# A gated cross-attention and mixture-of-experts block: routing and dispatch of the first mixture placed between the heads of the attention ahead of it

## The chip, the cores and the metric

One core of a Trainium2 chip runs the whole program. The time is device microseconds (us) of one execution; smaller is better. The kernel before took 1334.66 us in the median of three runs (1333.32 to 1339.74). Engines are called PE (matrix product), DVE (vector), ACT (scalar), POOL (GpSimd) and SP (which issues most DMAs).

## What is computed

The input `x` is 2048 tokens of 256 numbers (8 sequences of 256), with 512 context rows of 128. Four blocks follow each other, each added to `x` with a gate:

```python
x = x + tanh(g_xattn[0]) * L0_xattn(layernorm(x), ctx)   # 16 heads of 128, q and k RMS-normed, 64 keys a sequence
x = x + tanh(g_ffn[0])   * L0_ffn(layernorm(x))          # 64 experts, 8 per token, and a shared MLP
x = x + tanh(g_xattn[1]) * L1_xattn(layernorm(x), ctx)
x = x + tanh(g_ffn[1])   * L1_ffn(layernorm(x))          # 8 experts, every token through all
```

The change concerns the first two. The routing of `L0_ffn`, for each token, and the places of its rows at the experts:

```python
scores = sigmoid(x @ router.T); sc = scores + e_bias      # 64 experts in 8 groups
group_scores = top_k(sc by group, 2).sum(-1)              # best 4 of the 8 groups stay
topk_idx = top_k(masked sc, 8); topk_w = 2.5 * scores[topk_idx] / their sum
pos = running count of tokens per expert, in token order  # valid where pos < CAP
buf[expert, pos] = x[token]                               # [64, CAP, 256]
y = silu(buf @ w_gate) * (buf @ w_up) @ w_down            # per expert, inner size 88
out[token] += y[expert, pos] * topk_w;   out += shared_mlp(x)
```

CAP is 128 and the 2048 tokens make 256 choices per expert on average, so the places are filled by the earlier tokens, and most choices of the later half find none.

## The kernel before

The 2048 tokens lie in 16 tiles of 128 (partition = token), in 4 groups of 4 tiles. **First attention.** One step per group, i = 0 to 3. In a step PE goes through 16 heads: queries of the head (L1664, six 128x512 products in the split fp32r form), their squares summed for the norm (L1640), scores (L1649). DVE copies the queries out of PSUM (L707); ACT squares and rounds them; POOL subtracts to get the low part `q_lo` (L468), which L1640 reads. The softmax of the group before (DVE L641 to L664, exp on ACT) lies between the heads, and so does its product with the values (L1619). At the end of a step, behind head 15, PE computes for the next group the keys (L1555), the values times `Wo` (L1583, 32 products of 128x256), the token transposes (L1592) and the transposes of the normed keys (L1563). DVE copies the keys (L604), squares them (L610) and sums the squares (L612). The steps are a loop; the order inside one is written out by hand, and every engine follows it through ring counters (a bank of PSUM is filled, read, given back).

**First mixture.** After step 3 the rest of the attention of group 3 and the layer norms are done, then, group by group, the router logits, the routing on DVE (about L779 to L876, each operation over 4 tiles at once, 128x256), and the shared MLP on PE (L1708, L1728). The normed rows and the 64 weights of each token go to a table in DRAM (L379). The places of the tokens are then found per expert from keys: `largest` (L901, L904) takes the 8 greatest of a row of keys and strikes them out, 16 times over 1024 keys and 16 times over 256 candidates. Index arithmetic gives `src_now` and `dst_now`. The experts follow: 8 steps of 4 quarters q, 2 experts in each. For a quarter SP loads `w_gu`, `w_dn` (L383, L384), POOL gathers the 128 rows of each expert from the table (L479, an indirect DMA per expert), PE transposes them (L1750) and multiplies (L1764, L1777), ACT and DVE work between, and POOL adds the results to sums in DRAM (L489, an accumulating indirect DMA per expert). An accumulating DMA waits for the one before it to the same sum to have landed; there are two sums. When all are added, SP loads the sums (L418) and the second attention starts; from there on the two programs are alike.

## Time and profile before

| | |
|---|---|
| median of three runs | 1334.66 us (1333.32 to 1339.74) |
| the profiled execution, its own time | 1336.93 us |
| span in its profile | 1335.2 us |
| busy over the span | PE 1038.4 us (78%), DVE 697.9 (52%), ACT 431.5 (32%), POOL 278.2 (21%) |
| bytes moved by DMA | 66.36 MB |
| chain that ended last | PE 54%, DVE 14%, issue 12%, DMA 6%, ACT 6%, POOL 6% |

The stages of the span, as the views of the trace give them: up to 33.6 us first loads and preparation; heads of steps 0 to 3 from 33.6, 100.4, 186.6 and 272.6, each followed by its step's end; 337 to 470 the rest of the attention, routing, shared MLP; 470 to 530 the places; 543.0 the first addition to the sums and 744.2 the first load of them; from there the second attention and the second mixture up to 1335 us. An average over the span mixes these, so each part of the change has to be read in its own stage.

### The profile page before, as it was taken

To read this page: it belongs to the slowest core of one execution; us is meant where nothing else is said; L and a number is where in the kernel's file an instruction comes from. 1 tells how busy PE (TensorE), PEld (TensorE's weight loads), DVE (VectorE), ACT (ScalarE), POOL (GpSimd) and SP (SyncE) were. 2 spreads that over 40 slices of the span, in tenths; PEclk is the share of its full clock that TensorE was granted. 3 is DMA by queue.
4 is the path that set the end of the run, shared out by engine and by line. 5 is a ranking of instruction groups with operands and counts; after the bars stand their busy time and mean duration, and the time that the engine had idled before them with its cause. 6 is when DMAs were issued, how large, how long until landed. Compare 5 with 4: busy or idle time off the path is not lost.

```text
span 1335.2 us, 16322 instructions
## 1 busy us (share of the span) xinstructions
PE 1038.4 (78%) x5301; PEld 855.8 (64%) x5301; DVE 697.9 (52%) x1659; ACT 431.5 (32%) x793; POOL 278.2 (21%) x223
## 2 busy tenths in 40 slices
PE   5989979989766400776667368887989999999997
PEld 3867858778545300665556226564657989898996
DVE  6277586675758897222223477575675324232221
ACT  4565465554623100111111032324252232322221
POOL 0414214133000001788787110010100000000000
PEclk8999999999887655888787566757666999899899
DMA  7004000000001040788786540000000000000001
GB/s 266 3 0 137 1 1 1 0 1 1 1 0 40 24 126 11 170 173 180 166 186 120 144 164 1 2 0 0 0 0 0 1 1 0 0 0 0 0 0 64
DMA packets 58967, 66.36 MB, mean 50 GB/s; under 512 B 5037, under 2 KB 55719, under 8 KB 58151
## 3 DMA queue, kind: packets, MB, share of 16 engines
q1 hardware_dynamic: 45268, 46.48, 11.1%
q0 software_dynamic: 12288, 18.88, 8.1%
q8 instruction: 28, 0.46, 0.1%
q10 hardware_dynamic: 1363, 0.37, 0.1%
q14 instruction: 20, 0.16, 0.0%
HBM read 48.13 MB, written 17.56 MB: 49 GB/s over the span
## 4 chain that ended last, share of the span: by engine, by line
PE 54%; DVE 14%; issue 12%; DMA 6%; ACT 6%; POOL 6%; ACTq 0%; DVEq 0%; POOLq 0%; SPq 0%
PE bank L1959 12%; PE bank L1978 7%; DMA acc<-y,dst_now 5%; PE bank L1619 4%; PE bank L1664 4%; PE bank L1887 3%; PE bank L1845 3%; PE bank L1649 3%; POOL acc L489 2%; PE bank L1970 2%; POOL xg L479 2%; PE bank L1904 2%; POOL q_lo L468 2%; DVE cand L901 1%; PE bank L1804 1%
## 5 line engine op out<-in xcount | busy, mean ns | idle before, releaser
L1959 PE MATMUL bank<-gu_hi,xnT_split 128*128 128x352 f32 x640 | 158.7, 328 | 0.0
L468 POOL TENSOR_TENSOR q_lo<-soft,q_hi 128x512 fp32r<-128x512 f32 x64 | 93.2, 1456 | 236.8 <-ACT soft L1313 236.7
L1959 PEld LDWEIGHTS bank<-gu_hi,xnT_split 128*128 128x128 f32 x640 | 112.6, 190 | 1.0 <-issue 0.7
L479 POOL DMA_INDIRECT xg<-table,src_now x64 | 63.9, 999 | 216.5 <-DVE src_now L927 197.4
L489 POOL DMA_INDIRECT acc<-y,dst_now x64 | 102.3, 1599 | 26.7 <-issue 20.3
L1959 PE MATMUL bank<-gu_lo,xnT_split 128*128 128x352 f32 x320 | 103.8, 324 | 0.0
L1183 DVE SCALAR_TENSOR_TENSOR soft<-sg,combine_w,bank 128x176 f32<-128x176 f32 x160 | 56.4, 395 | 87.4 <-PE bank L1959 81.3
L1978 PE MATMUL bank<-dn,attnT 128*128 128x256 f32 x448 | 101.2, 384 | 0.0
L1978 PEld LDWEIGHTS bank<-dn,attnT 128*128 128x128 f32 x448 | 85.6, 194 | 11.2
L707 DVE COPY qT<-bank 128x512 f32<-128x512 f32 x64 | 44.2, 691 | 87.7 <-PE bank L1664 86.6
L1517 ACT ACTIVATE sg<-bank 128x352 f32<-128x352 f32 x80 | 37.1, 464 | 152.0 <-PE bank L1959 151.9
L947 DVE TENSOR_SCALAR y<-bank,xg 128x256 f32<-128x256 f32 x64 | 28.0, 480 | 106.6 <-PE bank L1777 106.6
L627 DVE SCALAR_TENSOR_TENSOR x<-bank,gates,x 128x256 f32 (+1 forms) x48 | 22.7, 482 | 114.0 <-PE bank L1978 94.8
L1764 PEld LDWEIGHTS bank<-xgT,w_gu 128*88 128x88 f32 x512 | 75.8, 193 | 6.7 <-issue 3.8
L1764 PE MATMUL bank<-xgT,w_gu 128*88 128x128 f32 x512 | 77.3, 316 | 0.7 <-issue 0.7
L1750 PE MATMUL bank<-ident,xg 128*128 128x128 f32 x128 | 25.7, 335 | 65.5 <-DMA xg<-table,src_now 65.5
L1309 ACT ACTIVATE q_hi<-qT 128x512 fp32r<-128x512 f32 x64 | 40.4, 630 | 91.3 <-DVE qT L707 91.2
L1619 PE MATMUL bank<-vw,attnT 128*128 128x256 f32 x256 | 62.1, 399 | 4.3 <-ACT attnT L1263 4.3
L1649 PE MATMUL bank<-kT,qT 128*128 128x64 f32 x512 | 64.0, 268 | 0.0
L1649 PEld LDWEIGHTS bank<-kT,qT 128*128 128x128 f32 x512 | 62.5, 191 | 1.4
L1750 PEld LDWEIGHTS bank<-ident,xg 128*128 128x128 f32 x128 | 17.4, 169 | 70.1 <-DMA xg<-table,src_now 56.5
L1959 PEld LDWEIGHTS bank<-gu_lo,xnT_split 128*128 128x128 f32 x320 | 60.7, 190 | 0.3
(256 smaller groups left out, 2140.1 us busy)
## 6 DMA issues: line engine op xcount, KB each, us to landing
w_gu<-in_L_ffn_w_gu SPq DMA_DIRECT2D x32, 352.0 KB
w_dn<-in_L_ffn_w_down SPq DMA_DIRECT2D x32, 176.0 KB
acc<-zeros SPq DMA_DIRECT2D x2, 2176.0 KB, 11.4
acc_rows<-acc SPq DMA_DIRECT2D x8, 512.0 KB, 4.9
gu<-in_L_gu SPq DMA_DIRECT2D x1, 3520.0 KB, 13.7
table<-xw SPq DMA_DIRECT2D x4, 640.0 KB
wo<-in_L_xattn_Wo SPq DMA_DIRECT2D x2, 1024.0 KB, 16.2
wq<-in_L_xattn_Wq SPq DMA_DIRECT2D x1, 2048.0 KB, 18.5
```

Of the source, the lines that this page charges most:

```text
L468: pool.tensor_tensor(q2_lo[:, h % 3, :], q2[h % 2], q2_hi[:, h % 3, :], ALU.subtract).then_inc(q2_split, 1)
L479: pool.indirect_dma_start(xg[:, q, e, :], None, table, bass.IndirectOffsetOnAxis(ap=src_now[:, q, e:e + 1], axis=0)).then_inc(xg_loaded[q] ...
L489: pool.indirect_dma_start(acc[e], bass.IndirectOffsetOnAxis(ap=dst_now[:, q, e:e + 1], axis=0), y[:, q, e, :], None, compute_op=ALU.add).t ...
L707: dve.tensor_copy(qT[:, h % 3, :], qr.read(dve)[:]).then_inc(q_ring.free, 1)
L1183: ins = dve.scalar_tensor_tensor(out=act_v[:, j % 2, at:at + F1], in0=sg[:, (j + p) % 2, e * F1:(e + 1) * F1], scalar=combine_w[:, j, 2 * ...
L1619: mm = pe.matmul(o_banks[0][:, 0:DIM], attnT[:, j % 2, p, :], vw[:, j // 2, p, :], start=(p == 0), stop=(p == 7))
L1649: mm = pe.matmul(s_bank[0][:, at:at + SKV], qT[:, h % 3, j * P:(j + 1) * P], kT[:, h, (j // 2) * SKV:(j // 2 + 1) * SKV], start=True, stop ...
L1664: mm = pe.matmul(b[:], w[:, c, h * D0:(h + 1) * D0], v[:, c, :], start=(n == 0), stop=(n == len(terms) - 1))
L1750: mm = pe.transpose(b[:, at:at + P], xg[:, q, e, c * P:(c + 1) * P], ident[:])
L1764: mm = pe.matmul(b[0:I0, e * P:(e + 1) * P], w_gu[:, q, e, c, o:o + I0], xgT[:, q % 2, e, c, :], start=(c == 0), stop=(c == C - 1))
L1959: mm = pe.matmul(b[:, 0:2 * F1], v[:, c, j * P:(j + 1) * P], w[:, c, p, o, :], start=(n == 0), stop=(n == len(terms) - 1))
L1978: mm = pe.matmul(o_banks[j % 2][:, 0:DIM], attn_flat[0:n, f, :], dn1[0:n, f, :], start=(f == 0), stop=(f == FC - 1))
```

## The change

The work of routing and of sending rows moves into steps 1 to 3 of the first attention, in batches of tiles (`BATCHES`: [0], [1,2], [3,4], ... [13,14], [15]), as soon as a tile's attention is done.

- **Routing** on DVE works on one or two tiles (128x64 or 128x128 per operation) in pieces `ln_*`, `choose1`, `choose2`, `choose3`, `place`, put between the softmax pieces at given heads (`ROUTE_EARLY`, `ROUTE_LATE`). Batches 0 to 4 are so treated in steps 1 to 3 (the last place of them behind step 3), batches 5 to 8 after step 3.
- **Places**: for each tile PE multiplies the chosen-expert matrix by a triangular matrix (`earlier`), plus ones times what earlier tiles took. DVE turns this into 8 row numbers per token, in a table of 64 x 128 rows. `largest` and the index arithmetic go.
- **Sending**: POOL stores the 128 rows of a tile 8 times, each by an indirect DMA of 128 rows x 1284 B: 128 stores in all. A row carries the normed token, the 64 weights and the token's number. In the program's order 24 stand in step 2, 21 in step 3, 83 behind it. A choice that found no place gets a row number beyond the table, which the store leaves out. Before a second use of its slots, `place` waits for the stores of two batches ago, and tiles from the ninth on share a counter with the tile 8 before. The table (10.5 MB) is filled with zeros first, by four DMAs of SP from step 0 on.
- **Experts**: no gathers. SP loads the 2 x 128 rows of a quarter by one ordinary DMA, 4 quarters ahead; the token number in the row gives the destination of the addition. The weights are laid out so that a partition's part lies in one piece in DRAM (2816 and 2048 B, where it was 704 and 1024 B). The accumulating DMAs stay as they are.
- **Steps**: the values move from the step's end into heads 0, 1, 3 and 5 of the next step (now read out of PSUM by ACT), the key transposes behind head 1. ACT takes the squares of the keys, reading PSUM, with a sum; L604, L610, L612 go. `q_lo` and its partner have two buffers where they had three. The steps are written out, not a loop.
- **Shared MLP**: after the last `place`, in products 512 wide; its inputs are stored to DRAM and loaded back transposed by SP.

```diff
-ROW = DIM + E0
+TOKEN = DIM + E0
+ROW = TOKEN + 1
...
+BATCHES = [[0]] + [[2 * n - 1, 2 * n] for n in range(1, NT // 2)] + [[NT - 1]]
...
+def early(i):
+    return 2 * (i - 1)
+def late(i):
+    return 2 * i - 1
...
+ATTN_TURNS, ATTN_OUTS, VALUE_TURNS = {5: 0, 8: 1, 12: 2, 15: 3}, {6: 0, 9: 1, 13: 2}, {0: 0, 1: 2, 3: 4, 5: 6}
...
+            if i and h == 1:
+                keys_across(i)
+            if i and h in ATTN_TURNS:
+                attn(i - 1, ATTN_TURNS[h])
+            if h >= 2 and h % 2 == 0:
+                s.append(("scores", i, (h - 2) // 2))
+            if i and h in VALUE_TURNS:
+                values(i - 1, VALUE_TURNS[h], 2)
+            if h == 7 and i + 1 < NG:
+                context(i + 1)
+            if i >= 2 and h == 7:
+                t.append(("place", late(i - 1)))
+            if i >= 2 and h == 0:
+                t.extend([("rows", late(i - 1)), ("place", early(i - 1))])
+            if i >= 2 and h == 2:
+                t.append(("logits", late(i - 1)))
+            if i and h == 11:
+                t.append(("rows", early(i)))
+            if i and h == 13:
+                t.append(("logits", early(i)))
+        if i + 1 < NG:
+            tokens(i + 1)
+        s.append(("scores", i, 7))
+        if i + 1 < NG:
...
-        table = nc.dram_tensor("table", (T + 1, ROW), F32, kind="Internal").ap()
+        table = nc.dram_tensor("table", (E0 * CAP, ROW), F32, kind="Internal").ap()
...
+            sp.wait_ge(q_ring.full, q_turn.at["query", 0, 6] + 1)
+            sp.wait_ge(blank_ready, 2)
+            table_d = table.rearrange("(e p) r -> p e r", p=P)
+            for n in range(4):
+                each = E0 // 4
+                sp.dma_start(table_d[:, n * each:(n + 1) * each, :], blank.unsqueeze(1).to_broadcast(
+                    [P, each, ROW])).then_inc(blank_stored, 16)
...
+            sp.wait_ge(s_ring.full, s_turn.at["scores", NG - 1, 7] + 1)
+            load_shared(0)
+            load_shared(1)
+            for q in range(4):
+                load_experts(0, q)
+            store_normed(5)
+            store_normed(6)
+            load_shared(2)
+            store_normed(7)
+            store_normed(8)
+            load_shared(3)
+            for n in range(8):
+                sp.wait_ge(row_stored[n], 16 * K0 * 2)
+            for q in range(4):
+                load_rows(0, q)
             for e in done1.values():
...
-                    sp.wait_ge(y_full, 4 * i + q - 3)
+                    sp.wait_ge(y_ready, 4 * i + q - 3)
+                    load_rows(i, q)
                     load_experts(i, q)
...
+            def split_squares(i, h):
+                pool.wait_ge(q2_ready, H0 * i + h + 1)
+                if H0 * i + h >= 2:
+                    pool.wait_ge(normed_head, H0 * i + h - 1)
+                pool.tensor_tensor(q2_lo[:, h % 2, :], q2[h % 2], q2_hi[:, h % 2, :],
+                                   ALU.subtract).then_inc(q2_split, 1)
...
+            def send_rows(b, lo, n):
+                for at in range(lo, min(lo + n, K0 * len(BATCHES[b]))):
+                    j, k = at // K0, at % K0
+                    t = BATCHES[b][j]
+                    pool.sem_inc(pool_wait_done, 1)
+                    pool.indirect_dma_start(table, bass.IndirectOffsetOnAxis(ap=slots[:, b % 2, j, k:k + 1], axis=0),
+                                            rows(t), None, bounds_check=E0 * CAP - 1,
+                                            oob_is_err=False).then_inc(row_stored[t % 8], 16)
...
+            FIRST, AFTER = {2: 1, 3: 2, 4: 1, 5: 2, 6: 2, 7: 2, 8: 1, 9: 2, 10: 2, 11: 1}, {12: 1, 13: 2, 14: 1, 15: 1}
+            for i in range(NG):
+                sent = {0: 0, 1: 0}
                 for h in range(H0):
-                    pool.wait_ge(q2_ready, H0 * i + h + 1)
-                    pool.tensor_tensor(q2_lo[:, h % 3, :], q2[h % 2], q2_hi[:, h % 3, :],
-                                       ALU.subtract).then_inc(q2_split, 1)
-
-            with pool.Fori(0, NG) as i:
-                split_squares(i)
+                    split_squares(i, h)
+                    if i >= 2:
+                        for part, (b, turns) in enumerate(((early(i - 1), FIRST), (late(i - 1), AFTER))):
+                            if h in turns:
...
+            for b in range(TAIL, len(BATCHES)):
+                number_rows(b)
+                send_rows(b, 0, 2 * K0)
...
-            def gather(i, q):
-                pool.sem_inc(pool_wait_done, 1)
-                for e in range(2):
-                    pool.indirect_dma_start(xg[:, q, e, :], None, table, bass.IndirectOffsetOnAxis(
-                        ap=src_now[:, q, e:e + 1], axis=0)).then_inc(xg_loaded[q], 16)
...
+            def place(b):
+                n = len(BATCHES[b])
+                w = slice(0, n * E0)
+                ch.wait()
+                t_turn.emptied(dve, ("place", b))
+                at = placed[:, w]
+                ch.add(dve.scalar_tensor_tensor(out=eq[:, w], in0=at, scalar=CAP - 0.5, in1=sel[:, w], op0=ALU.is_lt,
+                                                op1=ALU.mult))
+                ch.add(dve.tensor_tensor(tile_of(oth, n), place0[:].unsqueeze(1).to_broadcast([P, n, E0]),
+                                         tile_of(at, n), ALU.subtract))
+                ch.wait()
+                ch.add(dve.tensor_tensor(eq[:, w], eq[:, w], oth[:, w], ALU.mult))
+                ch.wait()
+                for j in range(n):
+                    ch.add(dve.max(top[:, j, :], tile_of(eq, n)[:, j, :]))
+                ch.wait()
+                if b >= 2:
+                    for t in BATCHES[b - 2]:
+                        dve.wait_ge(row_stored[t % 8], 16 * K0 * (t // 8 + 1))
+                dve.tensor_scalar(slots[:, b % 2, 0:n], top[:, 0:n], -1.0, float(E0 * CAP), ALU.mult,
+                                  ALU.add).then_inc(slots_ready, 1)
...
+            SOFT = {0: (by_norm, 0, maximum, 0), 1: (shift, 0, by_norm, 1), 2: (maximum, 1, shift, 1),
+                    3: (sums, 0), 4: (divide, 0), 5: (sums, 1), 6: (divide, 1, by_norm, 2),
+                    7: (maximum, 2, shift, 2, attended, 0), 8: (by_norm, 3, maximum, 3), 9: (sums, 2),
+                    10: (divide, 2, attended, 1), 11: (shift, 3), 13: (sums, 3), 14: (divide, 3, attended, 2)}
+            ROUTE_LATE = {1: (place, -1), 3: (choose1, 0), 4: (choose2, 0), 5: (choose3, 0), 9: (place, 0)}
+            ROUTE_EARLY = {8: ln_stats, 9: ln_roots, 10: ln_apply, 13: choose1, 14: choose2, 15: choose3}
...
-            def largest(dst, src):
-                for r in range(CAP // 8):
-                    sl.add(dve.max(dst[:, 8 * r:8 * r + 8], src))
-                    sl.wait()
-                    if r < CAP // 8 - 1:
-                        sl.add(dve.match_replace(src, dst[:, 8 * r:8 * r + 8], src, 0.0))
-                        sl.wait()
-            largest(cand[:, 0:CAP], keyT[:])
-            dve.drain().then_inc(cand_ready, 1)
-            dve.wait_ge(cand_moved, 16)
...
+                    for k in range(4):
+                        v = b[:, k * D0:(k + 1) * D0]
+                        ins = act.activation(v, v, ACT.Square, accum_out=kstat[:, 0, 4 * n + k:4 * n + k + 1])
+                    ins.then_inc(q_ring.free, 1)
...
+            def place(b):
+                pe.wait_ge(sel_ready, b + 1)
+                ps = t_turn.fill(pe, ("place", b))
+                for j in range(len(BATCHES[b])):
+                    terms = [(earlier, sel[:, j * E0:(j + 1) * E0]), (ones, taken[:, b % 2, :])]
+                    if j:
+                        terms.append((ones, sel[:, 0:E0]))
+                    for k, (m, v) in enumerate(terms):
+                        mm = pe.matmul(ps[:, j * E0:(j + 1) * E0], m[:], v, start=(k == 0),
+                                       stop=(k == len(terms) - 1))
+                mm.then_inc(t_ring.full, 1)
...
-    laid_out["L0_ffn_w_gu"] = np.concatenate([inputs["L0_ffn_w_gate"], inputs["L0_ffn_w_up"]], axis=2)
+    w_gu = np.concatenate([inputs["L0_ffn_w_gate"], inputs["L0_ffn_w_up"]], axis=2)
+    laid_out["L0_ffn_w_gu"] = w_gu.reshape(E0 // 2, 2, C, P, 2 * I0).transpose(0, 3, 1, 2, 4).reshape(E0 // 2, P, -1)
+    laid_out["L0_ffn_w_down"] = np.asarray(inputs["L0_ffn_w_down"]).reshape(E0 // 2, 2, I0, DIM).transpose(
+        0, 2, 1, 3).reshape(E0 // 2, I0, -1)
```

Four pieces show what moves in the order. On PE, the end of a step before (behind the last scores of head 15; `ctxV`, `soft` are the context rows' values and the normed keys of the next group):

```order
L1619 MATMUL bank<-vw,attnT 128x256 x8
L1555 MATMUL bank<-wk,ctxK 128x512 x4
L1682 MATMUL bank<-ident,n_rows 128x16 x4
L1583 MATMUL bank<-wo,ctxV 128x256 x16
L1592 MATMUL bank<-ident,xn 128x128 x8
L1563 MATMUL bank<-ident,soft 128x128 x16
L1551 MATMUL bank<-ident,ctx_rows 128x128 x2
L1664 MATMUL bank<-xnT_top,wq_hi 128x512
```

and the same place in step 1 of the change:

```order
L1965 MATMUL bank<-kT,qT 128x64 x4
L1851 MATMUL bank<-ident,xn 128x128 x8
...
L1965 MATMUL bank<-kT,qT 128x64 x4
L1868 MATMUL bank<-vw,attn1T 128x256 x8
L1812 MATMUL bank<-wk,ctxK 128x512 x4
L2006 MATMUL bank<-ident,n_rows 128x16 x4
L1942 MATMUL bank<-xnT_top,wq_hi 128x512
```

The values (L1583, there L1842), and the key transposes (L1563) are no longer between the last scores (L1649, there L1965) and the next step's first queries (L1664, there L1942); the token transposes have gone up among the heads.

On DVE, heads 3 and 4 of step 2 of the change (L1050 is the copy of a head's queries, L855 to L864 the softmax, L933 to L955 `choose1`; `q_full` is counted by PE, `t_free` stands for a PSUM bank, `dve_chain` for the operation before):

```order
L1050 COPY qT<-bank 128x512 [waits q_full]
L855 TENSOR_REDUCE small<-raw 128x16 [waits exp_done]
L857 RECIPROCAL small<-small 128x16 [waits dve_chain]
L933 TENSOR_SCALAR sig<-e_neg 128x128 [waits t_free,dve_chain]
L935 RECIPROCAL sig<-sig 128x128 [waits dve_chain]
L937 TENSOR_TENSOR sc<-sig,e_bias 128x128 [waits dve_chain]
L898 TENSOR_REDUCE of<-sc 128x16 [waits dve_chain]
...
L955 TENSOR_TENSOR of<-of 128x16 [waits dve_chain]
L1050 COPY qT<-bank 128x512 [waits q_full]
L864 TENSOR_TENSOR soft<-raw,small 128x1024
```

Twelve operations of routing now stand between two copies of queries, where the order before has only softmax pieces between them.

On POOL, heads 7 to 15 of step 2 and the first three of step 3 (L646 is the subtraction that gives `q_lo`, L670 an indirect store of rows; before, the 64 subtractions followed each other with nothing between them):

```order
L646 TENSOR_TENSOR q_lo<-soft,q_hi 128x512 [waits normed_head,q2_ready] x6
L657 IOTA rows_a 128x1 x2
L670 DMA table<-rows_a,slots 8192x321 [waits token_ready,slots_ready]
L646 TENSOR_TENSOR q_lo<-soft,q_hi 128x512 [waits normed_head,q2_ready]
L670 DMA table<-rows_a,slots 8192x321 x2
L646 TENSOR_TENSOR q_lo<-soft,q_hi 128x512 [waits normed_head,q2_ready]
L670 DMA table<-rows_a,slots 8192x321
L646 TENSOR_TENSOR q_lo<-soft,q_hi 128x512 [waits normed_head,q2_ready]
L670 DMA table<-rows_a,slots 8192x321 x12
L646 TENSOR_TENSOR q_lo<-soft,q_hi 128x512 [waits normed_head,q2_ready] x3
```

Stores now stand between a head's subtraction and the next one's, twelve of them between the steps.

## Rows read from the trace of the kernel before

**Rows 1.** Windows: stretch and length, each engine's busy us, PE clock, DMA share, GB/s.

```profile
33.60:100.40 66.80, 60.61 (x361) 47.27 (x359) 32.59 (x72) 38.05 (x77) 20.61 (x16) 1.00 0.01 2
100.40:186.60 86.20, 79.39 (x455) 63.39 (x455) 59.15 (x103) 45.44 (x88) 24.21 (x16) 0.99 0.16 54
186.60:243.30 56.70, 54.41 (x325) 45.69 (x326) 37.42 (x50) 27.46 (x49) 22.19 (x15) 0.99 0.00 1
243.30:272.60 29.30, 25.45 (x130) 18.52 (x128) 20.81 (x49) 17.08 (x37) 2.01 (x2) 0.95 0.00 0
272.60:337.00 64.40, 62.19 (x385) 52.89 (x384) 37.72 (x47) 31.06 (x54) 24.18 (x16) 1.00 0.00 1
337.00:398.00 61.00, 41.30 (x179) 32.02 (x178) 41.80 (x95) 26.57 (x46) 0.00 (x0) 0.84 0.00 0
398.00:469.80 71.80, 41.49 (x166) 31.92 (x164) 61.67 (x225) 21.18 (x29) 0.00 (x0) 0.67 0.12 40
469.80:529.70 59.90, 0.37 (x1) 0.18 (x1) 54.20 (x102) 0.22 (x1) 0.00 (x0) 0.50 0.22 59
543.00:744.20 201.20, 129.86 (x725) 113.49 (x723) 51.24 (x163) 29.28 (x60) 158.40 (x120) 0.80 0.78 163
```

**Rows 2.** Timeline of PE, end of step 1: start, length, what, idle before.

```profile
255.79 1.99 PE L1583 MATMUL bank<-wo,ctxV 128*128 128x256 f32 x8
258.26 7.52 PE L1583 MATMUL bank<-wo,ctxV 128*128 128x256 f32 x24 [0.48 <-ACT vw L1254]
269.29 3.62 PE L1563 MATMUL bank<-ident,soft 128*128 128x128 f32 x16 [2.64 <-ACT xnT L1270]
```

**Rows 3.** DVE by line, 186.6 to 272.6 us: busy us, mean ns, idle before.

```profile
L604 DVE COPY soft<-bank 128x512 f32<-128x512 f32 x4 | 2.8, 692 | 5.1 <-PE bank L1555 5.1
L612 DVE TENSOR_REDUCE kstat<-attnT 128x16 f32<-128x2048 f32 x1 | 2.3, 2287 | 0.0
L610 DVE TENSOR_TENSOR attnT<-soft 128x2048 f32<-128x2048 f32 x1 | 2.3, 2286 | 0.0
```

**Rows 4.** DVE by line, 398 to 470 us, operations of the routing.

```profile
L850 DVE MAX8 soft<-soft 128x8 f32<-128x64 f32 x16 | 2.4, 213 | 0.6 <-DVE soft L846 0.3
L797 DVE TENSOR_TENSOR soft<-soft 128x256 f32<-128x256 f32 x4 | 1.7, 426 | 0.1
L843 DVE TENSOR_TENSOR soft<-soft 128x32 f32<-128x32 f32 x4 | 0.8, 192 | 0.1
```

**Rows 5.** PE by line, 398 to 470 us, the shared MLP.

```profile
L1708 PE MATMUL bank<-xnT,sh_gu 128*88 128x256 f32 x48 | 14.6, 473 | 0.0
L1728 PE MATMUL bank<-sh_dn,sh_h 88*128 88x256 f32 x32 | 9.7, 430 | 13.6 <-DVE x L627 12.7 <-DVE sh_h L749 0.9
```

**Rows 6.** DVE by line, 469.8 to 527 us, the places.

```profile
L901 DVE MAX8 cand<-keyT 128x8 f32<-128x1024 f32 x16 | 19.6, 1228 | 1.5 <-ACT keyT L1361 1.0
L904 DVE MATCH_REPLACE8 keyT<-cand,keyT 128x1024 f32<-128x1024 f32 x15 | 18.1, 1208 | 0.0
```

**Rows 7.** Views of tiles `xg`, `acc`, `y`: ns min/median/max, first and last start; landing.

```profile
L1750 PE MATMUL bank<-ident,xg x128: 272/273/477, 534.1 to 726.6; 128*128 128x128 f32 x128
L479 POOL DMA_INDIRECT xg<-table,src_now x64: 949/983/1149, 529.7 to 723.3; - x64
L489 POOL DMA_INDIRECT acc<-y,dst_now x64: 1559/1586/1738, 543.0 to 740.3; - x64
DMA to landing us min/median/max: 3.8/4.3/5.8
```

**Rows 8.** Timeline of POOL near the experts' end.

```profile
713.46 1.74 POOL L489 DMA_INDIRECT acc<-y,dst_now  x1 [0.30 <-issue]
733.81 1.56 POOL L489 DMA_INDIRECT acc<-y,dst_now  x1 [1.20 <-issue]
735.67 1.56 POOL L489 DMA_INDIRECT acc<-y,dst_now  x1 [0.30 <-issue]
738.46 1.56 POOL L489 DMA_INDIRECT acc<-y,dst_now  x1 [1.23 <-issue]
```

**Rows 9.** Timeline of DVE and POOL in step 2.

```profile
197.05 1.23 DVE L650 TENSOR_TENSOR raw<-raw,small 128x1024 f32 x1
197.16 2.28 POOL L468 TENSOR_TENSOR q_lo<-soft,q_hi 128x512 fp32r<-128x512 f32 x1 [0.95 <-ACT soft L1313]
```

1365 lines of the change are left out of this document (774 added, 591 removed).

## Prediction

> **What bounds the kernel now.** I read the page first, then windows by stage, then one view inside each stage. The chain of the page gives PE 54%, which hides that the stages differ. In the heads of step 2 PE is busy 54.4 of 56.7 us, at step 3 62.2 of 64.4; DVE has 19 and 27 us free there, and between two steps PE still works 25.5 of 29.3 us [rows 1]. The first attention is PE's. From 398 to 469.8 us DVE is busy 61.7 of 71.8 us at a PE clock of 0.67, and from 469.8 to 529.7 us DVE works almost alone, 54.2 us, PE 0.4 [rows 1]: 130 us in which routing and places hold everything. The experts from 543.0 to 744.2 us are POOL's and the DMA engines': POOL 158.4 of 201.2 us, DMA share 0.78 [rows 1]. 0.5% of this kernel, 6.7 us, is about what a measurement can tell from no change.
>
> The profiled execution took 1336.93 us for a span of 1335.2; the median of runs is 1334.66, 2.3 below it. I add up in span time, put the 1.7 back for the execution, and take 2.3 off for the median.
>
> **A. Steps 1 to 3 get longer.** Each of the three steps takes into its heads: the values, 2.0 + 7.5 = 9.5 us and with the gap of 0.5 inside them 9.9; the key transposes, 3.6 [rows 2]; and new PE work of one early and one late batch (token transposes, logits in split products, places), 4 tiles, which I estimate at 5 us as of the size of the token and key transposes of a step. Head 1 now waits for the keys' norm, which used to run beside the values: the chain ACT squares, DVE root, ACT scaling comes to about 5 us by my estimate, from the two 2.3 us DVE operations that do the same work today [rows 3]. So heads go from 56.7 to about 80 us. The step's end loses values and key transposes (13.5 us) but gains that DVE comes to it late: `choose3`, roots and `apply` stand at heads 10 to 15, ahead of the squares' and softmax's share. 29.3 becomes about 22, where the plain difference would be 16. A step of 86 becomes 102 us: step 1, with no late batch yet, 98 (from 100.4 to 198), step 2 to 300, and the heads of step 3, today 64.4, take 88 to 388 where it was 337: **51 us later**. Ends: 3 x 9 + 3 = 30 us, if DVE and POOL fit into gaps and the moved PE work only moves (new PE 5, norm wait 4, a step); 65 us if the step's end keeps its 29.3 us in two of three.
>
> On POOL one or two stores now stand between a head's subtraction and the next one's, and PE's norm product waits for that subtraction. Step 2 asks 22 us for subtractions [rows 1] and at most 1.9 for each of 24 stores (below), 68 of 102 us; it fits, and what two stores in a row delay (2.8 us in a head of 5) lies in the same bounds. DVE has to fit in these heads too: two batches of two tiles. An operation on 256 elements takes 0.43 us, one of 32 0.19 and MAX8 0.21 [rows 4], so one of 128 between them, about 0.3. Twelve in `choose1`, nine in `choose2`, nine in `choose3`, five in `place`, and the norm: 13.9 us a batch, 28 a step. DVE's 37.4 + 28, less the 7.4 of the removed key copies and squares [rows 3], is 58 of 80 us: it fits by sum, but a piece of 3.3 us delays a query copy at which PE's ring waits. That is within the bounds above.
>
> **B. Behind step 3.** Removed: routing of all groups in 337 to 470, `largest` (19.6 and 18.1 us [rows 6], and half as much again on 256), index arithmetic, the round of gathers. Left on DVE: the softmax of group 3 and batches 5 to 8 (7 tiles, 4 x 14 less a tile), and the fifth place: 388 + 4 + 80 busy + 15 of waits on PE's logits and places = 487 for the last place. The shared MLP, now behind it, costs PE 14.6 x 4/3 + 9.7 = 29 us in four groups at 256 wide [rows 5]; at 512 wide I take 6.7 a group, 27 us, so 514. Then, as today from the first transposes of rows at 534.1 to the first addition at 543.0 [rows 7], 9 us: **first addition at 523** instead of 543.0.
>
> POOL's path runs beside it. 83 stores stand behind step 3. The trace has no such store. The lower bound is the gather, 0.98 + 0.30 of gap, 1.3 us; the upper one the accumulating store, 1.59 + 0.30, 1.9 us [rows 7, 8]. A plain store has the gather's form turned round, so I take 1.4. From 378, the last subtraction, some 10 us before the heads of step 3 end: 378 + 83 x 1.4 = 494; then 15 for landing (4.3 [rows 7]), loading of the rows, and the 9 to the first addition: 509. It is covered by the 523 of PE's path, with 14 us to spare. SP issues the shared MLP's loads and the first weights ahead of its wait for all stores, and the rows behind it, so nothing else is held there.
>
> **C. Experts.** 32 quarters; today 31 periods from the first addition at 543.0 [rows 7] to the last pair at 738.46 [rows 8], 6.3 us each. POOL spends 2 x (0.98 + 0.30 + 1.59 + 0.30) = 6.34: POOL is the bound, without a gap. With the gathers gone POOL's part is 3.8 us. Late in the stage, where gathers have ended, the pairs start 4.65 us apart (733.81, 738.46) [rows 8]: that is an addition's issue and its landing of 4.3 us [rows 7], and it is the chain that comes next. The DMA engines' work is 0.78 x 201.2 / 32 = 4.9 us a quarter [rows 1]; the gathers' bytes are the same when SP loads them. I take 5.3 between 4.65 and 6.3, since a DMA share of 0.92 (4.9 of 5.3) lengthens each landing. With 5.4 from the last pair's start to 743.9, just ahead of the first load of the sums at 744.2,, 31 x 5.3 + 5.4 = 170: **end at 693** instead of 743.9.
>
> By the chain alone (4.65 us) the stage would end 20 us sooner than that, at 673, and the kernel take 1264; I don't go there because the 4.9 us of DMA work is a floor that no other issuer lifts.
>
> The Trainium skill, "DMA: Bandwidth & Descriptors", section on SWDGE, HWDGE and iDMA, speaks against a large gain here: issuing engines are not queues of their own, all reach the same 16 DMA engines, and another issuer saves only issue time on its sequencer. The trace agrees so far as the DMA share is 0.78 with POOL as the issuer of all rows.
>
> **Zero fill.** 10.5 MB more are written in step 0 and 1, when the DMA share is 0.01 and 0.16 [rows 1]: hidden; the cover would fail only if a load of step 1 stood behind it. The layout of the weights (2816 B pieces) counts in C, within its bounds. ACT gets value reads and squares, some 10 us a step, on 45 busy of 86 in step 1 [rows 1]: hidden, but it is in the norm's chain above.
>
> **Sum.** 743.9 - 693 = 51 us earlier: 20 from B against A (543.0 to 523), 31 from C. Everything behind is unchanged: 1335.2 - 51 = 1284.4, plus 1.7 for the execution 1286, and on the median **1284 us**.
>
> **Rivals.**
> 1. *Better than that (0.17).* The steps cost 30 us in place of 51, stores 1.3, period 4.65: first addition at 502, end at 502 + 31 x 4.65 + 5.4 = 652, 92 us sooner: 1242 us. For it: DVE idles a third of each step [rows 1]. Against: PE idles only 2 us, and in-order queues lose time at each new wait.
> 2. *A store costs as an addition (0.14).* 378 + 83 x 1.9 = 536, + 15 + 170 = 721: 1312 us. It decides from 1.6 us on. For it: both write scattered rows of over 1 KB from SBUF. Against: an accumulation reads too.
> 3. *The experts' period stays (0.07).* DMA or the landing of additions bounds, 6.3 us: 523 + 195 + 5.4 = 724: 1315 us. For it: DMA share 0.78. Against: the end of the stage [rows 8].
> 4. *Slower: DVE holds POOL's stores up (0.12).* Behind step 3 DVE is nearly always busy, with operations on SBUF alone. At 197.16 POOL's subtraction takes 2.28 us, beside a DVE operation of 1.23 us with two inputs that began at 197.05 [rows 9], against 1.29 on average in the heads of step 0, 20.61 us for 16 [rows 1]. If every store waits out one such operation, it costs 1.3 + 1.2 = 2.5: 378 + 83 x 2.5 = 585.5, + 15 + 170 = 771, 27 us later than today: 1361 us. The point is 2.2 us a store: 378 + 83 x 2.2 + 185 = 746. Against it: even the longest additions take 1.74 in place of 1.59 [rows 7, 8] with DVE at work beside them, and most routing operations are 0.3 us long.
>
> The Trainium skill, "SBUF — State Buffer", on the two sides and the port pair that DVE and GpSimd share, calls this an exclusive lock, and gives about 3.1 us for a descriptor-writing DMA beside DVE's fast modes where it is 0.6 alone. By that figure the stores would take 83 x 3.4 = 282 us and the kernel about 1436 us. The trace agrees for the subtraction, and not for the additions.
>
> **How the numbers follow.** Forecast 0.50, rivals 0.17, 0.14, 0.07, 0.12. Faster by over 0.5%: 0.50 + 0.17 + 0.12 + 0.04 = 0.83; rivals 2 and 3 give 0.05 to within 0.5%, where they meet steps 65 us longer; slower 0.12. Low end 1240, rival 1. High end: steps +65 (14 more), stores 1.9, period 6: 392 + 158 + 15 + 31 x 6 + 5.4 = 756, 13 later or 1347; I put 1345. Above it lies rival 4.
>
> **What would show it.** Right: heads of steps 1 to 3 near 80 us with PE waiting at head 1 for the keys' norm; stores of 1.1 us with gaps of 0.3; PE busy with the shared MLP until about 514 while the last stores land; period of the additions 5.3 us at a DMA share over 0.85. Wrong: POOL busy to beyond 520 us with PE idle (rivals 2, 4, told apart by whether a store's length follows DVE's); period over 6 (rival 3); a step of over 107 us.

## The result, and the profile after

The changed kernel takes **1356.22 us** in the median of four runs (1354.58 to 1359.71), the kernel before 1336.29 in the runs beside it. The ratio is 1.015 (95% interval 1.012 to 1.019): 20 us slower, where I had forecast 51 faster (1284 against 1334.66). The profiled execution took 1354.58 us for a span of 1352.7.

| | before | forecast | after |
|---|---|---|---|
| first queries of step 1 | 100.4 | 100 | 94.5 |
| step 1, step 2 | 86.2, 85.9 | 98, 102 | 105.4, 119.8 |
| step 3, to the last norm behind its heads | 337 | 388 | 423 |
| last place on PE | 527 | 487 | 527 |
| first addition | 543.0 | 523 | 569.0 |
| period of the additions | 6.3 | 5.3 | 6.1 |
| last addition landed, sums loaded | 744 | 693 | 764 |

The mark for step 3 is PE's transposes of the last norm (L1682 at 337.4 before, L2006 at 422.8 after). Two expectations below count step 3 of the change only to its last scores at 418.1 and so have 98 us for it, where this mark gives 103.

Windows of the profile after, in the columns of [rows 1]: steps 1, 2 and 3 with its last norm; the tail to POOL's long wait for slots, the tail to its last store; the experts.

```profile
94.50:199.90 105.40, 83.98 (x460) 67.73 (x460) 66.10 (x157) 52.61 (x126) 23.27 (x16) 0.91 0.05 19
199.90:319.70 119.80, 92.96 (x493) 75.04 (x492) 85.27 (x210) 54.08 (x130) 47.50 (x43) 0.86 0.11 38
319.70:422.80 103.10, 87.01 (x478) 72.82 (x477) 78.13 (x185) 45.89 (x95) 49.03 (x46) 0.88 0.12 40
422.80:477.00 54.20, 26.17 (x118) 20.84 (x118) 34.95 (x94) 16.35 (x35) 22.77 (x28) 0.72 0.21 70
477.00:553.50 76.50, 47.40 (x167) 29.95 (x165) 50.92 (x179) 10.21 (x19) 56.32 (x61) 0.78 0.14 42
569.00:764.10 195.10, 127.69 (x726) 112.44 (x724) 46.79 (x136) 29.28 (x60) 98.83 (x64) 0.80 0.71 168
```

Against [rows 1], PE's 493 products of step 2 take 93.0 us where 455 took 79.4 in step 1 before, and its granted clock is 0.86 of full speed on average, not 0.99. Part of the 93.0 is new work, but the slower clock is seen on the same products too. First eight token transposes behind PE's longest wait, then eight of them in the step's end before, where PE had hardly waited:

```profile
304.02 1.97 PE L1851 MATMUL bank<-ident,xn 128*128 128x128 f32 x8 [9.19 <-DVE xn L816]
```

```profile
265.61 1.04 PE L1592 MATMUL bank<-ident,xn 128*128 128x128 f32 x8
```

The granted clock is 0.50, the lower of its two levels (1.2 GHz), from 304.0 to 305.6 us; ahead of the wait, from 290.0 to 294.8, and again from 307.8 it is 1.00 (2.4 GHz). So a wait costs twice: its own length, and slower products behind it. The waits of PE in step 2 (us in total, times, longest); in step 1 of the kernel before the same view adds up to 6:

```profile
PE bank L1851 <- DVE xn L816: 9.2, 1, 9.2
PE bank L1842 <- ACT raw L1515: 4.6, 2, 3.4
PE bank L1820 <- DVE soft L825: 3.1, 1, 3.1
PE bank L1860 <- DVE soft L864: 3.1, 2, 2.1
PE bank L1820 <- ACT kT L1479: 3.0, 1, 3.0
```

That is 9.2 us for the next group's normed tokens, 4.6 for PSUM banks that the moved values need and that ACT gives back with its copies of the scores (L1515), 3.1 for the keys' norm on DVE, 3.0 for ACT to read the transposed keys, and 3.1 for DVE's softmax.

The stores, by their two sources (ns min/median/max, first and last start), and their landing, the time from the issue of a DMA until its data are in place:

```profile
L670 POOL DMA_INDIRECT table<-rows_a,slots x64: 967/973/1712, 226.3 to 509.9; - x64
L670 POOL DMA_INDIRECT table<-rows_b,slots x64: 967/973/1602, 376.1 to 552.5; - x64
DMA to landing us min/median/max: 2.0/2.5/6.9
```

An indirect store's issue costs POOL 0.97 us in the median, and with the gap of 0.30 it is 1.27: the price of the gather in [rows 7], below the 1.4 that I took. The experts' additions, with what POOL waited for before them (us, times),

```profile
L700 POOL DMA_INDIRECT acc<-y,dst_now x64: 1542/1542/1596, 569.0 to 760.2; - x64
  DMA acc<-y,dst_now: 73.7, 29
```

and of `y`

```profile
DMA to landing us min/median/max: 3.7/5.0/7.6
```

POOL now waits 73.7 us, 29 times, for an addition that has not landed, and landing takes 5.0 us in the median where [rows 7] had 4.3. Nearly all of that waiting lies in the part of the stage in which weights are loaded; the last pairs start 4.5 us apart, as the last ones before did [rows 8]. The bound of this stage is no longer POOL's work but a chain of one addition behind the other.

Behind step 3, POOL:

```profile
453.92 0.97 POOL L670 DMA_INDIRECT table<-rows_a,slots  x1 [0.30 <-issue]
...
476.88 1.12 POOL L670 DMA_INDIRECT table<-rows_a,slots  x1 [21.75 <-DVE slots L1015]
...
552.52 0.97 POOL L670 DMA_INDIRECT table<-rows_b,slots  x1 [0.30 <-issue]
569.04 1.60 POOL L700 DMA_INDIRECT acc<-y,dst_now  x1 [15.55 <-DVE y L1168]
```

and PE:

```profile
439.73 8.81 PE L1842 MATMUL bank<-wvo,ctxV 128*128 128x256 f32 x24 [13.08 <-ACT vw L1488]
...
526.78 8.42 PE L1907 MATMUL bank<-sharedT,sh_gu 128*88 128x512 f32 x16
...
549.43 2.38 PE L1915 MATMUL bank<-sh_dn,sh_h 88*128 88x256 f32 x8 [0.24 <-DVE x L809]
...
559.16 1.09 PE L2060 MATMUL bank<-ident,xg 128*128 128x128 f32 x4 [7.35 <-POOLq L691]
```

and DVE:

```profile
450.23 0.23 DVE L933 TENSOR_SCALAR sig<-e_neg 128x128 f32<-128x128 f32 x1 [12.79 <-ACT e_neg L1548]
```

One wait goes through three engines. PE stands 13.1 us with the values half done, since ACT reads them only behind an exponential that needs DVE; DVE stands 12.8 us for the logits of batch 5, which PE has behind those values; POOL stands 21.8 us for slots. Then the last 56 stores run to 553.5. PE's shared MLP, 526.8 to 551.8, ends almost with them.

The 71 us between forecast and result lie in these places. The heads of step 3 with their last norm end 35 us later than I had them. From there to the last place it took 104 us, not 99; the shared MLP took 25, not 27; from its end to the first addition it took 17, not 9 (+11 together). And 31 periods of 6.1 in place of 5.3 are 25.

### The profile page after: what moved, and what is told of

Read it like the earlier page. It is cut to its first block, busy times and chain, and to the rows that moved or that the text cites. A ratio compares the mean times of both kernels' runs of the same rounds, so it can differ in the third digit from the quotient of the medians.

```text
span 1352.7 us, 16544 instructions
## 1 busy us (share of the span) xinstructions
PE 1056.2 (78%) x5330; PEld 866.5 (64%) x5330; DVE 675.5 (50%) x1753; ACT 440.7 (33%) x929; POOL 337.3 (25%) x305
## 4 chain that ended last, share of the span: by engine, by line
PE 52%; DVE 18%; DMA 12%; issue 7%; ACT 7%; POOL 2%; POOLq 1%; ACTq 0%; DVEq 0%; SPq 0%
DMA acc<-y,dst_now 12%; PE bank L2269 11%; PE bank L2288 7%; PE bank L1942 4%; PE bank L1868 3%; PE bank L2197 3%; PE bank L2155 3%; PE bank L1965 3%; PE bank L2280 2%; POOL table L670 2%; PE bank L2214 2%; PE bank L1957 2%; PE bank L1842 1%; PE bank L2188 1%; DVE newton L765 1%
## 5 line engine op out<-in xcount | busy, mean ns | idle before, releaser
L646 POOL TENSOR_TENSOR q_lo<-soft,q_hi 128x512 fp32r<-128x512 f32 x64 | 89.3, 1395 | 264.7 <-ACT soft L1526 264.6
L700 POOL DMA_INDIRECT acc<-y,dst_now x64 | 98.8, 1544 | 109.4 <-DMA acc<-y,dst_now 73.7
L2269 PE MATMUL bank<-gu_lo,xnT_split 128*128 128x352 f32 x320 | 103.6, 324 | 0.0
L2288 PEld LDWEIGHTS bank<-dn,attnT 128*128 128x128 f32 x448 | 85.7, 194 | 11.4
L1050 DVE COPY qT<-bank 128x512 f32<-128x512 f32 x64 | 44.0, 688 | 89.0 <-PE bank L1942 88.7
L2087 PE MATMUL bank<-w_dn,act_h 88*128 88x256 f32 x128 | 44.7, 481 | 49.2 <-DVE act_h L1158 48.4
L809 DVE SCALAR_TENSOR_TENSOR x<-bank,gates,x 128x256 f32<-128x256 f32 (+1 forms) x48 | 22.6, 481 | 108.6 <-PE bank L2288 95.1
L670 POOL DMA_INDIRECT table<-rows_a,slots x64 | 64.6, 1009 | 43.6 <-DVE slots L1015 24.2
L1868 PE MATMUL bank<-vw,attn1T 128*128 128x256 f32 x256 | 67.0, 420 | 3.3 <-ACT attn1T L1497 3.3
L670 POOL DMA_INDIRECT table<-rows_b,slots x64 | 63.8, 996 | 23.1 <-issue 16.8
L1965 PE MATMUL bank<-kT,qT 128*128 128x64 f32 x512 | 67.6, 278 | 0.0
L1965 PEld LDWEIGHTS bank<-kT,qT 128*128 128x128 f32 x512 | 66.4, 202 | 1.6
L2087 PEld LDWEIGHTS bank<-w_dn,act_h 88*128 88x128 f32 x128 | 26.1, 226 | 60.1 <-DVE y L1168 37.0
L722 POOL TENSOR_TENSOR k_blocks<-k1T,head_mask 128x512 f32<-128x512 f32 x16 | 16.2, 1042 | 192.4 <-ACT k1T L1669 192.4
```

Of the source, the lines that this page charges most:

```text
L646: pool.tensor_tensor(q2_lo[:, h % 2, :], q2[h % 2], q2_hi[:, h % 2, :], ALU.subtract).then_inc(q2_split, 1)
L670: pool.indirect_dma_start(table, bass.IndirectOffsetOnAxis(ap=slots[:, b % 2, j, k:k + 1], axis=0), rows(t), None, bounds_check=E0 * CAP - ...
L700: pool.indirect_dma_start(acc[e], bass.IndirectOffsetOnAxis(ap=dst_now[:, q, e:e + 1], axis=0), y[:, q, e, :], None, compute_op=ALU.add).t ...
L1050: dve.tensor_copy(qT[:, h % 3, :], q_turn.read(dve, ("query", i, h))[:]).then_inc(q_ring.free, 1)
L1868: mm = pe.matmul(o_banks[0][:, 0:DIM], attn1T[:, j % 2, p, :], vw[:, j // 2, p, :], start=(p == 0), stop=(p == 7))
L1965: mm = pe.matmul(s_bank[0][:, at:at + SKV], qT[:, h % 3, j * P:(j + 1) * P], kT[:, h, (j // 2) * SKV:(j // 2 + 1) * SKV], start=True, stop ...
```

## Experiments

The theories ahead of them were these. The steps grow because routing lies in DVE's queue ahead of what PE needs next, and because nothing on PE covers the keys' norm before the key transposes. The experts are bound by the additions' chain. The rivals were the moved values, the stores among the subtractions, and full DMA engines. Edits are against the changed kernel unless another is named, and the code shown is cut to the lines that matter. The period, the time of one quarter of two experts, is taken between the first and last start of the 64 additions, over 31.5.

### Four sums (`four_sums`)

```diff
-NA = 2
+NA = 4
-pool.wait_ge(acc_added[e], 16 * (4 * i + q))
+pool.wait_ge(acc_added[2 * (q % 2) + e], 16 * (2 * i + q // 2))
```

The additions go to `acc[2 * (q % 2) + e]`, so that each waits for the one two quarters back and not for the one before. DVE adds up four sums, and the load of `gu1` waits until they are read.

> Four sums in place of two, so that an addition waits for the one four additions back. Theory (the chain of additions bounds the experts): an addition to a sum now waits for the last one to it, whose landing takes 5.0 us in the median; with four sums that wait goes, and the period falls from 6.1 us to what the DMA engines need, 0.71 x 195 / 32 = 4.3, or POOL's 3.7: I expect 4.5 to 5.0 us, the experts 35 to 45 us shorter, less some 5 for loading and adding two more sums: 1316 to 1326 us. Rival (the DMA engines are full, landings only stretch): period 5.8 or more, time within 10 us of 1356.

1303.78 us (1296.69 to 1307.34); ratio to the kernel before 0.975 (0.972 to 0.978): 52 us less than the change. Window of the experts, waits and landing:

```profile
573.00:702.00 129.00, 106.92 (x727) 88.54 (x725) 47.41 (x136) 29.28 (x60) 99.02 (x64) 0.97 1.01 254
```

```profile
L701 POOL DMA_INDIRECT acc<-y,dst_now x64: 1542/1543/1717, 573.1 to 698.2; - x64
  DMA acc<-y,dst_now: 9.0, 14
```

```profile
DMA to landing us min/median/max: 3.8/7.0/7.7
```

125.1 / 31.5 = **4.0 us** a quarter, and the waits for additions are 9.0 us where they were 73.7. That is more than I expected. Landing itself takes 7.0 us now, but hardly anybody waits for it. PE's clock is 0.97 where it was 0.80. The chain is shown to have been the bound; full DMA engines were not. What holds the period at 4.0 was not told apart: the DMA share is 1.01, and POOL's own part, 2 x (1.54 + 0.30) = 3.7 us, is only 0.3 below.

### Four sums in the kernel before (`before_four_sums`)

> Four sums in the kernel before the change, everything else as it was. Theory (in the kernel before POOL's issues bound the experts at 6.34 us a quarter, and the chain of additions became the bound only when the gathers went): no gain, 1333 to 1340 us, the two more sums to load cost some us. Rival (the chain of additions bounded there too): 20 us or more less.

1341.25 us; ratio 1.004 (1.003 to 1.006). The experts:

```profile
544.70:741.50 196.80, 130.47 (x725) 114.20 (x723) 52.51 (x163) 29.29 (x60) 158.37 (x120) 0.79 0.80 166
```

POOL is busy for 158.4 us, as in [rows 1], and with 0.30 us of gap for each of its 120 issues that fills 194 of the 196.8. The stage is 4 us shorter than the 201.2 before, reading four sums in place of two takes 7 more (from the first to the last of their loads 26.5 us, where it was 19.2), and the kernel is 6 slower. So without the change four sums gain nothing: POOL was the bound there. With the change POOL's bound went, and the chain, which had become longer by its landing of 5.0 us, held the period at 6.1, only 0.2 below what it was.

### Weights loaded once (`weights_once`)

```diff
                     load_rows(i, q)
-                    load_experts(i, q)
```

> Leaves out the loads of the experts' weights from the second step on (all steps use the first eight experts' weights), 528 of some 849 KB that SP loads for a quarter. Theory (chain of additions, stretched by the loads beside it): landing falls from 5.0 to near the 3.8 of its minimum, the period from 6.1 to about 4.7, as in the last pairs of the kernel before; 40 us less. Rival (the chain of additions alone, whatever else the DMA engines do): the period stays at 6.1.

1330.24 us in one execution.

```profile
L699 POOL DMA_INDIRECT acc<-y,dst_now x64: 1542/1542/1596, 571.9 to 733.6; - x64
```

The period is 161.7 / 31.5 = 5.1 us, landing 3.9 in the median. Both expectations missed: not 4.7, not 6.1. In these two runs a period is the landing and 1.1 to 1.2 us (5.0 and 6.1; 3.9 and 5.1); in the last pairs before, with nothing beside them, it is 0.9 more than the shortest landing (3.8 and 4.65). The weights' loads beside the additions cost 1.0 us of the 6.1, the chain the rest.

### The weights' layout (`old_layout`)

On four sums, the layout of the weights before the change.

> Four sums, and the experts' weights in the layout of the kernel before (pieces of 704 and 1024 B in place of 2816 and 2048), nothing else. With four sums the DMA engines are full in the experts (share 1.0, period 4.0 us). Theory (the larger pieces take the DMA engines less time, and this is why a period of 4.0 is possible where my sum had 4.9 us of DMA work a quarter): the period rises to 4.5 to 5.0 us, 15 to 30 us in all. Rival (the size of the pieces doesn't matter here): period 4.0 to 4.2.

1304.77 us in one execution, beside 1303.78 with the new layout.

```profile
571.00:697.00 126.00, 108.51 (x745) 89.56 (x743) 47.92 (x137) 29.77 (x62) 93.93 (x61) 1.00 1.05 257
```

The period is 127.3 / 31.5 = 4.04. The theory is wrong: the size of the pieces does not matter here, even with the engines at 1.05 and 87,294 packets in place of 72,190. What makes a period under my 4.9 us possible is something else; the section on the prediction comes back to it.

### Routing made thin (`thin_routing`)

> Leaves out most of the routing arithmetic of batches 0 to 4 on DVE (choose1 and choose2 whole, choose3 but for four operations), some 8 us of DVE work for each batch, which then choose no expert; norms, products and stores stay. Theory (DVE's queue lengthens the steps, directly and through PE's clock, which falls when PE waits): step 2 falls from 119.8 us to 105 or less, step 3's heads from 98 to 85 or less, 30 us in all. Rival (the moved values and keys and the new PE work lengthen them): less than 10 us in all.

1329.63 us in one execution. Between the marks of PE's transposed norms, the steps take 99.2, 108.6 and 91.3 us, where the change has 105.7, 119.8 and 103.6: **30 us** less, as the theory had it, for about 40 us of DVE work left out. PE is busy 254 us in them where it was 264, for the same products: its clock is 0.93, 0.89 and 0.94 where it was 0.91, 0.86 and 0.88.

### Few stores in the steps (`few_stores_steps`)

> Leaves out 7 of the 8 stores of each of the tiles 0 to 6, so that 7 stores stand in steps 2 and 3 and the stretch behind them where 56 stood. Theory (routing in DVE's queue and the keys' norm lengthen the steps, the stores don't): steps 2 and 3 keep their length (119.8 and 98 to the end of the heads) within 4 us together. Rival (stores between the subtractions delay PE, or hold DVE's operations up): 10 us or more shorter.

1359.23 us in one execution; 105.5, 119.4 and 104.2 us between the same marks, unchanged. 49 stores fewer free no time in the steps. The rival falls: the stores in the steps are free.

### The tokens' norm early (`tokens_early`)

```diff
                             row_stats(i + 1)
-                        elif h == 15:
                             row_roots(EPS0)
```

> The norm of the next group's tokens (roots and apply) is done at head 12, beside its statistics, not behind the routing at head 15. Theory (the step's end waits for DVE, whose queue holds the routing's last piece ahead of the tokens): PE's waits of 7.6 and 9.2 us for the normed tokens go, the time falls by 14 to 20 us. Rival (PE waits for the same DVE work somewhere else): it falls by less than 5 us.

1346.83 us, 9 less; ratio to before 1.008 (1.006 to 1.011). The 9.2 us wait is gone, and 7 us of the 17 come back elsewhere: a wait of 3.6 us for ACT's transposed attention stands in step 2 that was not there. Half a success: between theory and rival.

### The values back at the step's end (`values_end`)

> The values go back to the step's end (steps 0 to 2), behind the keys, the rest stays. My prediction had this move at nothing. Theory (the move costs little, the routing in DVE's queue is what lengthens the steps): the waits for ACT at the values' banks, 3 to 5 us a step, go, and the end gets 10 us longer where the heads get as much shorter: within 8 us of 1356. Rival (the values between the heads are what costs): 15 us or more less.

1362.59 us (1359.12 to 1366.36), 6 more. The move of the values is indeed worth nearly nothing by itself, as I had it. But they stand behind the keys here while the norm is still asked for at head 1, so that they cover nothing; `both_ends` below moves the norm and the key transposes with them.

### Both, and values and keys at the end (`both`, `both_ends`)

`both` has four sums and the tokens' norm early. `both_ends` also moves the values, the key transposes and `key_norm` to the step's end:

```diff
+                if i + 1 < NG:
+                    values(i, 0, 8)
+                    transpose_keys(i + 1)
```

> Four sums and the tokens' norm at head 12 together. Theory (the two act in different stages and add up): 1303.8 less 9.4, so 1290 to 1299 us. Rival (the earlier start is eaten by something behind it): 1300 or more.

1286.61 us (1278.83 to 1288.29), 17 less than `four_sums`. The theory had 5 to 14, and the sum of the two parts is 9, so this is 8 more than they give by themselves, of which nothing here shows the reason. The rival, that the earlier start is eaten up, falls.

> As both, and the values and the key transposes of the next group go back to the step's end in steps 0 to 2, the keys' norm to DVE's end of the step, as in the kernel before: the values on PE cover the norm again. Theory (the moved key transposes cost their wait for the norm, 7 us a step, and the values' banks 3 to 5 us, with nothing won for it): 15 to 25 us less than both. Rival (DVE, full with routing at the step's end, does the keys' norm so late that PE waits for it there): within 8 us of both.

1273.19 us (1270.58 to 1278.35): 13 less than `both`, just under the theory's range. PE at the end of step 1:

```profile
184.61 0.60 PE L2002 MATMUL bank<-ident,n_rows 16*128 16x16 f32 x4
185.15 11.36 PE L1840 MATMUL bank<-wvo,ctxV 128*128 128x256 f32 x32
196.34 1.04 PE L1818 MATMUL bank<-ident,soft 128*128 128x128 f32 x8
198.64 1.23 PE L1818 MATMUL bank<-ident,soft 128*128 128x128 f32 x8 [1.26 <-ACT kT L1477]
199.63 0.48 PE L1940 MATMUL bank<-xnT_top,wq_hi 128*128 128x512 f32 x1
```

The values take 11.4 us and the keys' norm is ready behind them: of its wait 1.3 us is left. The heads of step 3 end 19 us earlier than in `both` (393.2 against 412.4), and so does the first addition start (539.6 against 558.6); where the 6 us between that and the 13 of the medians go is open.

### Fewer stores behind step 3 (`few_stores_tail`)

> Leaves out 7 of the 8 stores of each of the tiles 9 to 15. In the profile of the change POOL's last store is issued at 552.5 and PE ends the shared MLP at 551.8: two paths of one length. Theory: the first addition comes only 1 to 4 us earlier than 569.0, since PE's path holds it. Rival (the stores alone set it): 10 us or more earlier.

1350.10 us in one execution. The first addition starts at

```profile
L706 POOL DMA_INDIRECT acc<-y,dst_now x64: 1542/1542/1592, 563.1 to 753.6; - x64
```

The start at 563.1 is 6 us earlier, and 8 when its steps, 2 us longer, are counted. That lies between the two expectations. As I read it, PE's path and POOL's had nearly one length up to 552 us, but only behind POOL's last store come landing and the load of the rows. PE's path alone, 551.8 and the 9 us that I had taken, gives 561, and the start less those 2 us of steps is 561; so POOL's path held the first addition by 8 us, where the forecast gave it 14 to spare.

### Logits of batch 5 ahead of the last values (`both_tail`)

```diff
             place(4)
+            route(5)
             values(m, 0, 8)
-            route(5)
```

On ACT `scores_in1(5)` and `values_in` go ahead of the second exponential.

> As both, and behind step 3 PE does the logits of batch 5 ahead of the last values, and ACT reads them and the values ahead of the second exponential. In the profile of the change PE waits 13.1 us there with the values half done, DVE 12.8 us for these logits, and POOL 21.8 us for the next slots. Theory (one wait that all three engines pass on): the first addition comes 8 to 14 us earlier, and the time falls as much against both. Rival (DVE's work behind step 3 is the bound and only its idle time moves): less than 4 us.

1271.85 us (1266.17 to 1275.92), 15 less than `both`. POOL's waits for slots behind step 3 (total, times, longest), which were 27.5 us in `both`:

```profile
POOL table L671 <- DVE slots L1016: 11.6, 3, 7.2
```

The first addition starts 19 us earlier (539.7 against 558.6). Of these, 6 come from shorter steps, which this edit doesn't touch, so that some 13 are its own. The wait that three engines passed on was real and on the path.

### What is left of the steps (`thin_ends`)

> As both_ends, and leaves out most of the routing arithmetic of batches 0 to 4 as thin_routing did. Steps 1, 2 and 3 to the end of its heads took 86.2, 85.9 and 64.8 us before the change, 93.8, 107.6 and 86.0 in both_ends. Theory (DVE's queue and the keys' wait are the causes, new PE work the rest, some 5 us a step): 88, 95 and 75. Rival (the moved work makes PE wait in further places): each 5 us or more above that.

1246.18 us in one execution, 27 less than `both_ends`. From 105.57, the first queries of step 1, to those of steps 2 and 3 (PE's timeline):

```profile
194.53 0.48 PE L1952 MATMUL bank<-xnT_top,wq_hi 128*128 128x512 f32 x1
...
290.61 0.48 PE L1952 MATMUL bank<-xnT_top,wq_hi 128*128 128x512 f32 x1
```

These are 89.0 and 96.1 us, and 74.9 to the last norm at 365.5, where the theory had 88, 95 and 75. The growth of the three steps, from 236.9 to 328.3, is 91 us: the tokens' norm 7 (`tokens_early`), values and keys 34 (321 to 287 from `both` to `both_ends`, of which 14 go back to the end of step 0 and 19 are won), routing arithmetic 27 (287 to 260), and 23 are left for new PE work and what remains of waits, which no run tells apart.

### All parts, and the front end alone (`all_parts`, `two_sums_rest`)

> Four sums, tokens' norm at head 12, values and keys at the step's end, logits of batch 5 ahead of the last values. Theory (each part acts in its own stage): 1286.6 less 13.4 and less 14.8, so 1254 to 1264 us. Rival (the last stores or DVE behind step 3 hold the end once two waits are gone): 1267 or more.

**1259.33 us** (1258.10 to 1264.33); ratio to the kernel before 0.942 (0.940 to 0.944). This version beats both kernels, the change by 97 us and the one before by 76. Its experts have the length of those with four sums:

```profile
527.40:656.00 128.60, 108.31 (x725) 89.48 (x723) 48.63 (x136) 29.35 (x60) 98.80 (x64) 0.95 1.02 255
```

> The three parts of the front end alone (tokens' norm, values and keys, logits of batch 5), with two sums as in the change. Theory (the chain of additions costs 50 us whatever starts it): 45 to 55 us more than with all parts, 1305 to 1315, still faster than the kernel before. Rival (with an earlier start the experts' stage grows): 1325 or more.

1310.81 us (1309.20 to 1313.19); ratio 0.981 (0.978 to 0.984). With the front end mended and two sums the change does gain 25 us; the chain of additions costs 51 more, as in the change itself.

## Why the prediction was wrong

**Right:** routing and places off DVE's tail alone (54 us of `largest` gone); a store at the gather's price, at the lower end of my bounds; POOL's stores in the steps free; the shared MLP 25 us for 27; `values` worth nothing by themselves; DVE's 14 us a batch (about 14.5 for batch 7: norm 4.1, choosing 8.9, place 1.4). Rivals 2 and 4 fell as prices: stores cost 1.27 us, not 1.9 or 2.5. That the kernel came out slower, as in rival 4, is no merit of that rival, since its cause was another. Two of the signs of being wrong that I had named came: a step of over 107 us (119.8) and a period of over 6 (6.1).

**Step A is the largest miss** (35 of 71 us). I checked that DVE's work fits "by sum" into 80 us, 58 of them, and gave the order in its queue almost no price. Even the sum was short: the 7.4 us that I took off for L604, L610 and L612 ran at the step's end before (252.8 to 262.6), not among the heads, so that it is 65 of 80. But the order did the harm: `choose3` ahead of the tokens' norm cost a wait of 9.2 us, which I had named and put at 6 for the whole step's end. The keys' norm I had at 5 us; PE waited 6. The routing arithmetic cost 27 to 30 us of the steps in all (`thin_ends`, `thin_routing`), and moving the values and key transposes, with the norm left uncovered, 19 (`both_ends`). I also missed what the waits do to PE's clock, 0.99 before and 0.86 in step 2: PE was busy 264 us in three steps and 254 when the routing was thin, with the same products. Rows of before showed this price already, in the stages with waits: 0.84 and 0.67 from 337 to 470 [rows 1]. And I read DVE's idle third as room, although it comes in pieces, each behind a head's queries.

**Step B** missed by 11 us. "15 of waits" behind step 3 was a guess; the order of the tail, where logits stand behind values and values behind an exponential, gave it as a wait of 13 us on three engines, and `both_tail` took some 13 off with three moved lines. I also took POOL to run its 83 stores without a break from 378; it stood 27.5 us for slots, and started its last 56 only at 476.9. So its path ended 8 us behind PE's and not 14 ahead.

**Step C** is the third (25 us), and here the mechanism itself was half right. I had named the chain as the next bound, but took its length from the last pairs, 4.65 us [rows 8], when no weights are being loaded; in the stage it is 6.1. Rival 3, which I gave 0.07, came nearest in this stage: it had 6.3 for the period, and 6.1 was measured. The reason for 5.3, "4.9 us of DMA work is a floor", was wrong twice. The work is at most 4.0 us a quarter, since that period was reached; 0.78 x 201.2 counts engines as busy that wait, or work that direct loads of rows don't need, and which of these it is I did not test. And it was not the floor that mattered. The landings of 4.3 in [rows 7] stood close to the period of 6.3 all along: 4.3 and the 1.2 that a period needs beside the landing is an estimate of 5.5 for the chain before. Why landing rose to 5.0 and the period to 6.1 with the change is not shown; that SP now loads the rows together with the weights, in one burst, is my guess.

The Trainium skill ("DMA: Bandwidth & Descriptors", section on SWDGE, HWDGE and iDMA) has the rule that another issuer saves only issue time. This case agrees: POOL's issues of the gathers went, 2 x (0.98 + 0.30) = 2.6 us a quarter, and the stage became 6 us shorter in all, 201.2 to 195.1. What filled the engines was not the issuer but the number of additions in flight (share 0.71 with two sums, 1.01 with four).

The exclusive lock that the Trainium skill describes ("SBUF — State Buffer", section on the two separate sides) was rival 4. As a price it is nothing: both groups of 64 stores have a median of 973 ns, with DVE at work beside most of them. But the longest stores of the change do show it:

```profile
309.24 1.20 DVE L833 TENSOR_TENSOR xnT_rest<-xnT,xnT_top 128x1024 fp32r<-128x1024 f32 x1
309.59 1.71 POOL L670 DMA_INDIRECT table<-rows_a,slots  x1 [0.30 <-issue]
...
281.26 1.22 DVE L855 TENSOR_REDUCE small<-raw 128x16 f32<-128x1024 f32 x1 [0.21 <-ACT raw L1493]
281.64 1.00 POOL L670 DMA_INDIRECT table<-rows_a,slots  x1 [0.91 <-POOL rows_a L657]
```

Ten stores started within a DVE operation of 1.2 us with two inputs, 0.18 us or more before its end, and all ten ended 0.83 to 0.87 us behind that end; the longest are those at 309.59, 391.42 and 482.19, with 1.71, 1.60 and 1.49 us. Within a reduction, which has one input, a store keeps its 1.0. One store that started at almost the same time as such an operation, 0.02 us behind it, took 0.98. So the rival's mechanism exists, but such meetings are rare: the 10 stores of 128 that took more than 1.05 us lost 3 us together. The other way round it shows more often; see the last section.

## What to carry to other kernels

When a change removes the bound of a stage, price the chain behind it under the load of the stage, not at its quiet end: a dependent DMA's landing time and what its loop adds, against the period. If the chain is within some per cent of the present period, lengthen it first (more sums or buffers); here four sums in place of two were worth 51 us after the change and nothing before it. For work put "into the gaps" of a full engine's stage, read in its order what stands ahead of each thing that the full engine waits for, and count what every new wait costs by the clock.
